# Two layers of graph attention on one core: loads held behind the first x, and the last stage's row sent through memory

## Chip, cores and metric

The kernel runs on one core of one Trainium2 chip. The metric is the device time of one execution in microseconds. The time before is the median of three runs.

## What is computed

Two graph attention layers with a residual connection, on 8 graphs of 1024 nodes and 128 features, all in float32. The adjacency has one entry in 64 set, on average.

```python
def _L0_gnn_ref(h, adj, W, a):
    Wh = jnp.einsum('bni,io->bno', h, W)
    e = (Wh @ a1)[:, :, None] + (Wh @ a2)[:, None, :]
    e = jnp.where(e > 0, e, 0.2 * e)
    attention = jax.nn.softmax(jnp.where(adj > 0, e, neg), axis=2)
    return jax.nn.elu(jnp.einsum('bnm,bmo->bno', attention, Wh))
...
h = jnp.maximum(_layernorm(x, axis=-1), 0.0)
x = x + _L0_gnn_ref(h, adj, L0_gnn_W, L0_gnn_a)
h = jnp.maximum(_layernorm(x, axis=-1), 0.0)
x = x + _L1_gnn_ref(h, adj, L1_gnn_W, L1_gnn_a)
```

The second layer is the same without the elu, with a mask where adj is 0.

## The kernel before

**Stages.** A stage is one layer of one graph, so there are 16, n = 0 to 15. The order is layer 0 of graphs 0, 1, 2, then layer 1 of graph b and layer 0 of graph b + 3 in turn, then layer 1 of graphs 5, 6, 7. LAST is 15. Stages 3 and 15 are LATE (L44): their input x comes out of the stage only three before them.

**One stage.** The 1024 nodes are 8 tiles (t) of 128 rows. For stage n:

- `statistics` and `moments` on VectorE and `normaliser` on GpSimd (a power of -1/2) give the layer norm, `normalise` on ScalarE applies it, `transposes` on TensorE and `copy_hT` on ScalarE turn it (relu on the way).
- `project` multiplies by W, extended by the two columns W a1 and W a2 (`project_a`, `copy_wa`), and gives Wh and the two scores of every node in PSUM (`prj`). `copy_e` takes the scores, `spread_emax` on TensorE and `exp_args` on VectorE take the maximum over all nodes, `exps` on ScalarE the exponentials (`sqr`). `scale_wh` writes Wh into `wh`, scaled.
- The mask of tile t (`masks`, L668, VectorE, 128x1024) is max(row, scalar) min adj: it needs the **row** of the stage, 1024 values that are the same in every partition (`row_r`), a scalar for each partition and the adj tile. `attend` (L950, TensorE) multiplies the masked tile with `wh[t]` into three PSUM banks (`acc`), 8 blocks a tile; each block is two instructions in the trace, so 16 a tile and 128 a stage.
- `take_acc` (the drain, L677 and L687) copies the three banks out on VectorE and takes the reciprocal of the sums. Until bank k is copied, the next stage's first tile can't write it (`acc_copied`). `scale_accs` on ScalarE scales, `add_elu`, `add_x` or `add_hp` on VectorE add to x, and `store` writes layer 1's result out.

**The row.** There are two ways to make it. A stage in `SPREAD = (1, LAST)` uses `spread_r` (L907): eight transposes on TensorE, each of a column broadcast over 128, put the row into PSUM for all partitions, and `copy_row` on ScalarE (L411) copies it to `row_r` in two halves. Any other stage uses `turn_r` (L916), one transpose to 8 x 128, `copy_r` on ScalarE to `rT` (L419), and `load_row` on SyncE (L218): a DMA of 4 KB to memory, a wait until it has landed, and a DMA that reads it back 128 times, 512 KB.

**Order of the work.** Each engine's order is written out by hand. While TensorE works through `attend(n)`, the next stage is prepared between its tiles. For n = 14 the order on TensorE is (L993 to L1014): tile 0, transposes(15), tile 1, project(15), tile 2, spread_emax(15), tile 3, spread_r(15), tiles 4 to 7; then stage 15 with tiles 0 to 3 and `attend_last`, which takes tiles 4 to 7 bank by bank (L959, L965), so that the output leaves in five parts. On VectorE: masks 0 and 1 of stage 14, the drain of 13, masks 2 to 4, copy_e, mask 5, exp_args, the add of graph 5, masks 6 and 7; then (L808 to L813) masks 0 and 1 of stage 15, the drain of 14, masks 2 to 4, the add of graph 6, masks 5 to 7, and `last`. `before_drain(n)` (L188) gives the number of masks of stage n ahead of the drain of n - 1; it is also the tile after which `attend` releases `p_used` (L956).

**The start.** SyncE issues (L231 to L245) the first half of x of graph 0, the three loads of layer 0's weights (w_tr and w_ext, 64 KB each, a_cols, 1 KB), then x of graph 1 and 64 adj tiles of 512 KB with the other x between them. ScalarE's queue issues at the same time (L450 to L454) the second half of x of graph 0 and the three loads of layer 1's weights. TensorE first turns the identity 20 times (`keep_warm`), then `transposes_first`: four tiles that ScalarE has centred, project_a(0), four tiles that VectorE has centred. Then come `project_first`, `project_a(1)` (L974, waits for layer 1's weights), hsum_first of four tiles, spread_emax(0), and so on.

Of the kernel before, what the change touches and what calls it, by code (L numbers as in the profile page):

```python
# [18 lines left out]
def gat_two_layers(nc, x, adj, w0, w0t, a0, w1, w1t, a1, r_rows, out):  # L19
    B, T, _, N = adj.shape  # L20
    D = x.shape[2]
# [4 lines left out]
    HALF = T // 2  # L26
    AHEAD = 3
    X_SLOTS = 6
    LAST = 2 * B - 1
# [14 lines left out]
    LATE = tuple(stage_of[1, b] for b in range(B) if stage_of[1, b] - stage_of[0, b] == 3)  # L44


    SPREAD = (1, LAST)

# [2 lines left out]
    xv = x.rearrange("b (p t) d -> b p (t d)", t=T)  # L53
    ov = out.rearrange("b (p t) d -> b p (t d)", t=T)

    with ExitStack() as ctx:
# [14 lines left out]
        w_ext = sb("w_ext", [P, 2, E])  # L71
        w_tr = sb("w_tr", [P, 2, D])
        a_cols = sb("a_cols", [P, 2, 2])
        adj_sb = sb("adj_sb", [P, AHEAD * T * N], I32)
        x_sb = sb("x_sb", [P, X_SLOTS * T * D])
# [111 lines left out]

        def before_drain(n):  # L188

            return {1: 4, AHEAD: 1, LAST - 2: 3}.get(n, 2)  # L190

        def spread_rows(m):

# [12 lines left out]
        @block.sync  # L206
        def _(sp):
            def load_x(b):
                if b >= X_SLOTS:
                    sp.wait_ge(out_stored[b - X_SLOTS], 16)  # L210
                sp.dma_start(x_at(b), xv[b]).then_inc(x_in[b], 16)

            def load_adj(b, t):
                if b >= AHEAD:
                    sp.wait_ge(p_ready, T * stage_of[1, b - AHEAD] + t + 1)
                sp.dma_start(adj_at(b, t), adj[b, t]).then_inc(adj_in[b % AHEAD][t], 16)

            def load_row(m):  # L218
                k = loaded_rows(m)
                sp.wait_ge(rT_ready, k)  # L220
                sp.dma_start(r_rows, rT[:, :]).then_inc(r_written, 16)
                sp.wait_ge(r_written, 16 * k)
                sp.dma_start(row_r[:, m % 2, :],
                             r_rows.rearrange("t p -> (t p)").partition_broadcast(P)
                             ).then_inc(row_in, 16)

            def store(b):
                sp.wait_ge(hp_free, stage_of[1, b] + 1)
                sp.dma_start(ov[b], x_at(b)).then_inc(out_stored[b], 16)

            sp.dma_start(x_sb[:, 0:HALF * D], xv[0][:, 0:HALF * D]).then_inc(x_half, 16)  # L231
            sp.dma_start(w_tr[:, 0, :], w0t).then_inc(w_in[0], 16)
            sp.dma_start(a_cols[:, 0, :], a0).then_inc(w_in[0], 16)
            sp.dma_start(w_ext[:, 0, 0:D], w0).then_inc(w_in[0], 16)
            load_x(1)
            for t in range(HALF):
                load_adj(0, t)
            load_x(2)
            for t in range(HALF, T):
                load_adj(0, t)  # L240
            for t in range(T):
                load_adj(1, t)
            load_x(3)
            for t in range(T):
                load_adj(2, t)  # L245
            load_row(2)
            load_x(4)
            load_x(5)
            load_row(AHEAD)

            for n in range(AHEAD, LAST):
                l, b = stages[n]
                loads = l == 1 and b + AHEAD < B
                l_old, b_old = stages[n - 3]
                if l_old == 1 and b_old + X_SLOTS < B:
                    load_x(b_old + X_SLOTS)
                if loads:
                    for t in range(3):
                        load_adj(b + AHEAD, t)
                if n + 1 not in SPREAD:  # L260
                    load_row(n + 1)
                if loads:
                    for t in range(3, T):
                        load_adj(b + AHEAD, t)
                if stages[n - 1][0] == 1:
                    store(stages[n - 1][1])
            store(B - 2)
            for k, (lo, hi) in enumerate(last_parts):
                sp.wait_ge(last_ready, k + 1)
                sp.dma_start(ov[B - 1][:, lo * D:hi * D],  # L270
                             x_at(B - 1)[:, lo * D:hi * D]).then_inc(out_stored[B - 1], 16)
            for b in range(B):
                sp.wait_ge(out_stored[b], 16 * (len(last_parts) if b == B - 1 else 1))
# [60 lines left out]
        def _(act):  # L334
# [112 lines left out]
                    nc.scalar.activation(prj[:, k, 0:C], uniform[:, LAST % 2, :],  # L447
                                         ACT.Copy).then_inc(seeded_last, 1)

            half = slice(HALF * D, T * D)  # L450
            nc.scalar.dma_start(x_sb[:, half], xv[0][:, half]).then_inc(x_in[0], 16)
            nc.scalar.dma_start(w_tr[:, 1, :], w1t).then_inc(w_in[1], 16)
            nc.scalar.dma_start(a_cols[:, 1, :], a1).then_inc(w_in[1], 16)
            nc.scalar.dma_start(w_ext[:, 1, 0:D], w1).then_inc(w_in[1], 16)  # L454
            centre_first()
            copy_hT_first()
            exps_first()
# [51 lines left out]
        def _(dve):  # L509
# [145 lines left out]
            def masks(n, tiles):  # L655
                l, b = stages[n]
                for t in tiles:
                    if l == 0:
                        dve.wait_ge(adj_in[b % AHEAD][t], 16 * (b // AHEAD + 1))
                    if n == 0:  # L660
                        dve.wait_ge(row0_ready, 2)
                    elif t == 0:
                        dve.wait_ge(p_used, n)
                        if n in SPREAD:
                            dve.wait_ge(row_copied, 2 * spread_rows(n) + 2)
                        else:
                            dve.wait_ge(row_in, 16 * loaded_rows(n))
                    nc.vector.scalar_tensor_tensor(pbuf[:, t, :], row_r[:, n % 2, :],  # L668
                                                   sqr[:, n % 2, 0, t:t + 1], adj_at(b, t),
                                                   ALU.max, ALU.min).then_inc(p_ready, 1)  # L670
# [136 lines left out]
                    masks(n, (6, 7))  # L807
            masks(LAST, range(before_drain(LAST)))  # L808
            take_acc(LAST - 1)
            masks(LAST, (2, 3, 4))  # L810
            add_hp(B - 2)
            masks(LAST, (5, 6, 7))
            last()  # L813
# [2 lines left out]
        def _(pe):  # L816
# [175 lines left out]
            attend(0, (7,))  # L992
            for n in range(1, LAST):  # L993
                if n + 1 in LATE:
                    k = 1 if n + 1 in SPREAD else 2
                    attend(n, range(k))
                    transposes(n + 1)
                    attend(n, (k,))
                    project(n + 1)
                    attend(n, (k + 1,))  # L1000
                    spread_emax(n + 1)
                    attend(n, (k + 2,))
                    spread_r(n + 1) if n + 1 in SPREAD else turn_r(n + 1)
                    attend(n, range(k + 3, 6))
                else:
                    project(n + 1)
                    attend(n, (0,))
                    spread_emax(n + 1)
                    attend(n, (1, 2) if n + 2 in LATE else (1,))
                    turn_r(n + 1)  # L1010
                    attend(n, (3, 4, 5) if n + 2 in LATE else (2, 3, 4, 5))
                if n + 2 <= LAST and n + 2 not in LATE:
                    transposes(n + 2)
                attend(n, (6, 7))  # L1014
# [33 lines left out]
```

## Time and profile before

| | us |
|---|---|
| median of three runs | 298.88 (298.63 to 299.03) |
| the profiled execution | 298.75 |
| its span | 296.9 |
| what lies around the span | 1.85 |
| TensorE busy | 290.6 (98%) |
| VectorE busy | 268.1 (90%) |
| ScalarE busy | 167.3 (56%) |
| GpSimd busy | 48.5 (16%) |

The profiled execution ran 0.13 us under the median. Busy time is a sum over the span; the chain that ended last, followed back from the last instruction, tells which work set the end. Times in the rows are from the start of the span. "x16" is a count of instructions. TensorE's granted clock is recorded as 1.00 throughout.

### The profile page before, as it was taken

The numbers are of one execution on the slowest core, as the hardware profiler recorded it, in microseconds if no ns is written. First come the engines' busy times: TensorE is split into PE (matmuls) and PEld (weight loads), VectorE is DVE, ScalarE is ACT, GpSimd is POOL, SyncE is SP. The second block draws the span as 40 slices with busy tenths as digits, with TensorE's granted clock in tenths as the row PEclk, the third lists the DMA queues.
The fourth block names the chain that finished last, engine by engine and source line by source line (L and its number), as shares of the span: only waits on it lengthen the run. The fifth ranks groups of instructions, "written<-read, shape, count | busy, mean of one in ns | idle before, by whom it ended". The sixth has DMA issues, their size and how long they took to land.

```text
span 296.9 us, 6592 instructions
## 1 busy us (share of the span) xinstructions
PE 290.6 (98%) x2562; PEld 287.8 (97%) x2562; DVE 268.1 (90%) x613; ACT 167.3 (56%) x490; POOL 48.5 (16%) x53
## 2 busy tenths in 40 slices
PE   7999999999999999999999999999999999999996
PEld 7889999999999999999999999999999999999996
DVE  4796899889999989999899989999899989988796
ACT  3377482983856539382683737566393836384310
POOL 2712003205021120303003030210303000400000
PEclk9999999999999999999999999999999999999999
DMA  7999935004690347714584344903566110101012
GB/s 238 416 408 406 407 148 212 2 7 138 195 371 3 143 153 252 305 33 164 161 305 192 144 128 142 367 8 141 149 227 265 68 77 0 73 0 72 1 73 71
DMA packets 15215, 49.50 MB, mean 167 GB/s; under 512 B 2024, under 2 KB 3280, under 8 KB 15184
## 3 DMA queue, kind: packets, MB, share of 16 engines
q1 hardware_dynamic: 14608, 48.69, 44.4%
q8 instruction: 20, 0.33, 0.4%
q10 hardware_dynamic: 576, 0.39, 0.4%
q14 instruction: 11, 0.09, 0.1%
HBM read 44.83 MB, written 4.25 MB: 165 GB/s over the span
## 4 chain that ended last, share of the span: by engine, by line
PE 86%; DVE 7%; issue 2%; DMA 2%; ACT 2%; POOL 1%; DVEq 0%; POOLq 0%; ACTq 0%
PE acc L950 64%; PE prj L888 8%; PE tp L827 4%; DVE pbuf L668 3%; PE acc L965 2%; PE acc L819 2%; DMA row_r<-r_rows 1%; ACT xn L376 1%; DVE stats L563 1%; PE prj L891 1%; POOL rstd L281 1%; PE prj L860 1%; PE tp L910 1%; DVE accs L677 1%; PE prj L965 1%
## 5 line engine op out<-in xcount | busy, mean ns | idle before, releaser
L950 PE MATMUL acc<-wh,pbuf 128*128 128x129 f32 x1968 | 229.6, 275 | 0.9 <-DVE pbuf L644 0.3
L950 PEld LDWEIGHTS acc<-wh,pbuf 128*128 128x128 f32 x1968 | 225.1, 192 | 1.6 <-issue 0.9
L668 DVE SCALAR_TENSOR_TENSOR pbuf<-row_r,sqr,adj_sb 128x1024 f32<-128x1024 f32 x127 | 157.5, 1276 | 1.4 <-ACT row_r L416 1.0
L281 POOL TENSOR_TENSOR rstd<-vareps,neg_half 128x8 f32<-128x8 f32 x15 | 38.5, 2568 | 202.3 <-DVE vareps L581 202.2
L426 ACT ACTIVATE accs<-accs,rec 128x128 f32<-128x128 f32 x120 | 36.7, 389 | 51.0 <-DVE rec L687 51.0
L376 ACT ACTIVATE xn<-x_sb,shift,rstd 128x128 f32<-128x128 f32 x120 | 47.6, 478 | 0.0
L396 ACT ACTIVATE wh<-prj,wh 128x128 f32<-128x128 f32 x120 | 31.9, 357 | 0.0
L888 PE MATMUL prj<-w_ext,hT 128*128 128x130 f32 x240 | 29.3, 275 | 0.0
L888 PEld LDWEIGHTS prj<-w_ext,hT 128*128 128x128 f32 x240 | 28.0, 191 | 0.0
L382 ACT ACTIVATE hT<-tp 128x1024 f32<-128x1024 f32 x15 | 15.4, 1024 | 20.3 <-PE tp L827 20.3
L677 DVE TENSOR_TENSOR accs<-acc,uniform 128x387 f32<-128x387 f32 (+1 forms) x45 | 20.5, 506 | 2.9 <-PE acc L950 2.8
L563 DVE BATCH_NORM_STATS2 stats<-x_sb 128x6 f32<-128x128 f32 x112 | 22.9, 275 | 0.0
L827 PE MATMUL tp<-ident,xn 128*128 128x128 f32 x128 | 17.4, 277 | 0.3 <-DVE pbuf L668 0.3
L827 PEld LDWEIGHTS tp<-ident,xn 128*128 128x128 f32 x128 | 14.7, 142 | 1.0 <-DVE pbuf L668 0.4
L606 DVE COPY ecol<-prj 128x12 f32<-128x12 f32 x15 | 2.5, 167 | 10.8 <-PE prj L891 10.8
L373 ACT ACTIVATE act_gate<-shift 128x1 f32<-128x1 f32 x15 | 2.9, 192 | 14.1 <-POOL shift L284 14.1
L387 ACT ACTIVATE sqr<-args 128x24 f32<-128x24 f32 x15 | 3.3, 219 | 11.8 <-DVE args L640 11.8
L698 DVE TENSOR_TENSOR x_sb<-x_sb,ex 128x1024 f32<-128x1024 f32 x8 | 9.7, 1217 | 0.1
L692 DVE SCALAR_TENSOR_TENSOR ex<-accs,ex 128x1024 f32<-128x1024 f32 x8 | 9.7, 1218 | 0.0
L438 ACT ACTIVATE ex<-ex 128x1024 f32<-128x1024 f32 x8 | 8.5, 1058 | 0.3
L704 DVE TENSOR_TENSOR x_sb<-accs,x_sb 128x1024 f32<-128x1024 f32 x7 | 8.5, 1218 | 0.0
L436 ACT ACTIVATE ex<-accs 128x1024 f32<-128x1024 f32 x8 | 8.4, 1046 | 0.1
(105 smaller groups left out, 155.6 us busy)
## 6 DMA issues: line engine op xcount, KB each, us to landing
adj_sb<-in_adj SPq DMA_DIRECT2D x64, 512.0 KB, 6.5
row_r<-r_rows SPq DMA_DIRECT2D x13, 512.0 KB, 4.2
x_sb<-in_x SPq DMA_DIRECT2D x7, 512.0 KB, 6.4
out_x<-x_sb SPq DMA_DIRECT2D x7, 512.0 KB, 3.0
x_sb<-in_x ACTq DMA_DIRECT2D x1, 256.0 KB, 3.6
x_sb<-in_x SPq DMA_DIRECT2D x1, 256.0 KB, 3.4
r_rows<-rT SPq DMA_DIRECT2D x13, 4.0 KB
out_x<-x_sb SPq DMA_DIRECT2D x1, 192.0 KB, 1.9
```

Source lines behind the costliest of these rows:

```text
L281: nc.gpsimd.tensor_tensor(rstd[:, :], vareps[:, :], neg_half[:, :], ALU.pow).then_inc(rstd_ready, 1)
L376: nc.scalar.activation(xn[:, t, :], src[:, t, :], ACT.Identity, bias=shift[:, t:t + 1], scale=rstd[:, t:t + 1]).then_inc(xn_ready, 1)
L382: nc.scalar.activation(hT[:, :], tp[:, :], ACT.Relu, accum_out=hsum[:, :]).then_inc(hT_ready, 1)
L396: nc.scalar.activation(wh[:, m % 2, t, 0:D], prj[:, k, s * E:s * E + D], ACT.Copy, scale=wh[:, m % 2, t, D:C]).then_inc(wh_ready, 1)
L426: op = nc.scalar.activation(hp[:, t, :], hp[:, t, :], ACT.Copy, scale=rec[:, t:t + 1])
L563: st = nc.vector.bn_stats(stats[:, t, :], src[:, t, :])
L668: nc.vector.scalar_tensor_tensor(pbuf[:, t, :], row_r[:, n % 2, :], sqr[:, n % 2, 0, t:t + 1], adj_at(b, t), ALU.max, ALU.min).then_inc(p_ ...
L677: nc.vector.tensor_tensor(accs[:, k * NB:k * NB + w, :], acc[:, k, 0:w * C].rearrange("p (s c) -> p s c", c=C), uniform[:, e % 2, :].unsqu ...
L692: nc.vector.scalar_tensor_tensor(ex[:, :, :], hp, 0.0, ex[:, :, :], ALU.max, ALU.subtract).then_inc(hp_free, 1)
L827: return nc.tensor.transpose(tp[:, t * P:(t + 1) * P], xn[:, t, :], ident[:, :])
L888: nc.tensor.matmul(prj[:, k, s * E:(s + 1) * E], hT[:, t * P:(t + 1) * P], w_ext[:, l, :], start=(s == 0), stop=True, skip_group_check=True)
L950: mm = nc.tensor.matmul(sum_at(k, s), pbuf[:, t, i * P:(i + 1) * P], wh[:, n % 2, t, :], start=(t == 0 and s == 0 and k < NB), stop=(t == ...
```

## The change

It does two things. At the start, SyncE issues both halves of the first x, waits until the first has landed, and only then issues everything else; layer 0's weights move to ScalarE's queue and layer 1's to SyncE's, behind the first adj tile. At the end, stage 15 leaves `SPREAD`, so that its row goes through memory (turn_r, copy_r, load_row), and only one of its masks stands in front of the drain of stage 14. The position k = 1 of stage 15's preparation on TensorE is kept.

```diff
-    SPREAD = (1, LAST)
+    SPREAD = (1,)
...
-            return {1: 4, AHEAD: 1, LAST - 2: 3}.get(n, 2)
+            return {1: 4, AHEAD: 1, LAST - 2: 3, LAST: 1}.get(n, 2)
...
-            sp.dma_start(x_sb[:, 0:HALF * D], xv[0][:, 0:HALF * D]).then_inc(x_half, 16)
-            sp.dma_start(w_tr[:, 0, :], w0t).then_inc(w_in[0], 16)
-            sp.dma_start(a_cols[:, 0, :], a0).then_inc(w_in[0], 16)
-            sp.dma_start(w_ext[:, 0, 0:D], w0).then_inc(w_in[0], 16)
+            half = HALF * D
+            sp.dma_start(x_sb[:, 0:half], xv[0][:, 0:half]).then_inc(x_half, 16)
+            sp.dma_start(x_sb[:, half:2 * half], xv[0][:, half:2 * half]).then_inc(x_in[0], 16)
+
+            sp.wait_ge(x_half, 16)
             load_x(1)
             for t in range(HALF):
                 load_adj(0, t)
+                if t == 0:
+                    sp.dma_start(w_tr[:, 1, :], w1t).then_inc(w_in[1], 16)
+                    sp.dma_start(a_cols[:, 1, :], a1).then_inc(w_in[1], 16)
+                    sp.dma_start(w_ext[:, 1, 0:D], w1).then_inc(w_in[1], 16)
...
-            half = slice(HALF * D, T * D)
-            nc.scalar.dma_start(x_sb[:, half], xv[0][:, half]).then_inc(x_in[0], 16)
-            nc.scalar.dma_start(w_tr[:, 1, :], w1t).then_inc(w_in[1], 16)
-            nc.scalar.dma_start(a_cols[:, 1, :], a1).then_inc(w_in[1], 16)
-            nc.scalar.dma_start(w_ext[:, 1, 0:D], w1).then_inc(w_in[1], 16)
+            nc.scalar.dma_start(w_tr[:, 0, :], w0t).then_inc(w_in[0], 16)
+            nc.scalar.dma_start(a_cols[:, 0, :], a0).then_inc(w_in[0], 16)
+            nc.scalar.dma_start(w_ext[:, 0, 0:D], w0).then_inc(w_in[0], 16)
...
             masks(LAST, range(before_drain(LAST)))
             take_acc(LAST - 1)
-            masks(LAST, (2, 3, 4))
+            masks(LAST, range(before_drain(LAST), 5))
...
-                    k = 1 if n + 1 in SPREAD else 2
+                    k = 1 if n + 1 == LAST else 2
```

## Rows read from the trace of the kernel before

**Rows 1.** The page, part 4: the chain that ended last, by engine.
```profile
PE 86%; DVE 7%; issue 2%; DMA 2%; ACT 2%; POOL 1%; DVEq 0%; POOLq 0%; ACTq 0%
```

**Rows 2.** The chain in order of time, 260 to 297 us: start, duration, what.
```profile
271.81 0.87 PE tp L910 x8
272.68 8.49 PE acc L950 x76
...
286.98 5.51 PE acc L965 x48
```

**Rows 3.** Timeline, 246 to 297 us, VectorE: start, duration, instruction, idle before.
```profile
272.00 4.86 DVE L668 SCALAR_TENSOR_TENSOR pbuf<-row_r,sqr,adj_sb 128x1024 f32<-128x1024 f32 x4
...
278.82 1.49 DVE L677 TENSOR_TENSOR accs<-acc,uniform 128x387 f32<-128x387 f32 x3 [1.96 <-PE acc L950]
...
280.47 3.63 DVE L668 SCALAR_TENSOR_TENSOR pbuf<-row_r,sqr,adj_sb 128x1024 f32<-128x1024 f32 x3
...
285.15 3.67 DVE L668 SCALAR_TENSOR_TENSOR pbuf<-row_r,sqr,adj_sb 128x1024 f32<-128x1024 f32 x3
```

**Rows 4.** The chain in order of time, 40 to 52 us: the row of stage 2.
```profile
42.27 0.12 PE tp L918
...
42.71 1.21 DMA r_rows<-rT
...
43.94 4.35 DMA row_r<-r_rows
...
48.42 1.84 DVE pbuf L668 x2
```

**Rows 5.** Broadcast reads (L223), issue to landing: all 13; 100 to 160; 230 to 260.
```profile
DMA to landing us min/median/max: 3.4/4.2/4.8
...
DMA to landing us min/median/max: 4.2/4.2/4.3
...
DMA to landing us min/median/max: 3.4/3.4/3.5
```

**Rows 6.** Timeline, 26 to 78 us: the drain of stage 1 and what follows.
```profile
50.83 1.35 DVE L677 TENSOR_TENSOR accs<-acc,uniform 128x387 f32<-128x387 f32 x3
...
51.52 3.81 PE L950 MATMUL acc<-wh,pbuf 128*128 128x129 f32 x32 [0.21 <-DVE accs L677]
...
52.33 2.43 DVE L668 SCALAR_TENSOR_TENSOR pbuf<-row_r,sqr,adj_sb 128x1024 f32<-128x1024 f32 x2
```

**Rows 7.** Waits of SyncE: us in total, times, longest.
```profile
SPq L223 <- DMA r_rows<-rT: 14.0, 13, 2.2
```

**Rows 8.** Timeline, 0 to 26 us.
```profile
0.72 0.38 SPq L231 DMA_DIRECT2D x_sb<-in_x  x1
...
5.48 1.28 ACT L340 ACTIVATE xn<-x_sb,negmean 128x128 f32<-128x128 f32 x4 [1.59 <-DVE negmean L514]
...
8.63 0.29 DVE L549 BATCH_NORM_STATS2 stats<-x_sb 128x6 f32<-128x128 f32 x1
...
9.67 0.30 PEld L823 LDWEIGHTS acc<-a_cols,w_tr 128*128 128x128 f32 x2
```

**Rows 9.** DMA, 0 to 8 us: GB/s in slices of 0.2 us; issues, median us to landing.
```profile
GB/s 0 0 0 0 0 0 0 0 61 82 82 236 307 399 379 369 420 320 320 259 223 300 205 305 266 274 369 358 379 254 271 287 392 412 389 451 389 389 451 430
...
x_sb<-in_x ACTq DMA_DIRECT2D x1, 256.0 KB, 3.6
x_sb<-in_x SPq DMA_DIRECT2D x1, 256.0 KB, 3.4
...
w_ext<-in_w SPq DMA_DIRECT2D x1, 64.0 KB, 3.9
w_ext<-in_w ACTq DMA_DIRECT2D x1, 64.0 KB, 5.0
```

**Rows 10.** The page, part 6: the small stores of the output, us to landing.
```profile
out_x<-x_sb SPq DMA_DIRECT2D x3, 64.0 KB, 1.6
```

**Rows 11.** The adj load issued at 104.2 us on an idle queue, issue to landing.
```profile
DMA to landing us min/median/max: 3.3/3.3/3.3
```

## The prediction

> **What bounds the kernel now.** I read the page first: the chain that ended last is 86% TensorE, with VectorE next [rows 1]. So an edit pays only where that chain leaves TensorE, or if it takes work off TensorE. Then I read the chain in order of time. At the start it runs through the first x, VectorE, ScalarE and GpSimd. In stage 1 it leaves TensorE for the row of stage 2, which goes through memory. From stage 4 on it is TensorE alone, to the closing matmuls [rows 2]. The change touches the start and the end, so I read those two instruction by instruction.
>
> At the end two engines are level. In the last stage the closing matmuls (L965) need 48 x 0.112 = 5.37 us at the pace of the others (8.49 us for 76) and took 5.51: TensorE already waits some 0.14 us for the last mask [rows 2]. VectorE has an idle 1.96 us ahead of the drain of stage 14, and none between there and its last mask, which ends at 285.15 + 3.67 = 288.82 [rows 3]. A later last mask is a later end, one for one.
>
> **The change at its end: the row of stage 15.** It removes eight transposes (0.87 us of the chain) and puts one in (0.12 as stage 2's turn shows): TensorE reaches the end of stage 14 0.75 us earlier [rows 2, 4]. Two ScalarE copies of half a row become one over 8 partitions, on an engine that is not in the chain there: nothing.
>
> The row, until now copied out of PSUM, takes a round trip. Stage 2 shows each step: from the end of the tile ahead of the turn (42.27) through turn, copy, write (1.21) and broadcast read (4.35) to the first mask at 48.42, that is 6.15 us [rows 4]. In stage 14 the same tile ends at 271.81 [rows 2]. The read's time is the open term. It is 3.4 to 4.8 with a median of 4.2 over the 13 rows; three reads with a load or a store issued within 1 us behind them took 4.2 to 4.3, two with nothing so close took 3.4 and 3.5 [rows 5]. Here the store of batch 5, ready since the add that VectorE ends at 272.0, is queued behind load_row(15) and goes out right behind the read. I take 4.2: the row's mask starts at 271.81 + 6.15 - 0.15 = 277.81.
>
> VectorE has done its two last masks of stage 14 by 272.00 + 4.86/2 = 274.4 and then stands until 277.81, 3.4 us in place of 1.96 [rows 3]. From there its queue is fixed: one mask in front of the drain, 1.21 (half of the 2.41 from 48.42 to 50.83 in stage 2); drain and reciprocal, 1.50 (50.83 to 52.33) [rows 4, 6]; four masks and the add of batch 6, 4.68 (280.47 to 285.15 with three masks) + 1.21 = 5.89; three masks, 3.67 [rows 3]. Sum 12.27, so the last mask ends at 290.08 instead of 288.82: **+1.26 us**. TensorE starts stage 15 at 277.81 + 1.21 + 0.69 = 279.7 (as in stage 2, where the drain starts at 50.83 and TensorE at 51.52) [rows 6], against 272.68 + 64 x 0.112 = 279.83 before, so its 0.75 us is all but spent there. It then waits for mask 1 of stage 15, which has moved behind the drain, and again for the last one. The mask count in front of the drain changes only where TensorE waits; VectorE's total is the same with one or two.
>
> Bounds of this part: with the shortest read, 3.4, the drain waits for TensorE again, mask 1 starts at 280.47 - 0.75 = 279.72 and the last ends at 279.72 + 5.89 + 3.67 = 289.28, +0.46. With 4.8 it is 1.26 + 0.6 = +1.86. For the 13 writes SyncE waited 14.0 us in all, and 2.2 for one of them, 1.2 more than the mean [rows 7]; that would add another 1.2. Neither a gain nor zero comes out, because mask 1 moves behind the drain (1.21) and TensorE gives back only 0.75.
>
> **The change at its start: x alone in front.** The chain begins with the first half of x, issued at 0.72 [rows 8] and landed 3.4 us later. Its other half on ACT's queue, issued at the same moment, took 3.6: the two shared the engines [rows 9]. After the change what shares is w0t, 64 KB, since the second half follows on the same queue. That is 192 KB less ahead of its landing, at some 400 GB/s [rows 9] 0.5 us: it lands at 3.6. Bounds: zero below. Above, a 64 KB store took 1.6 and a single 512 KB load on an idle queue 3.3 [rows 10, 11]; in proportion 256 KB takes 2.33 and lands at 3.05, a gain of 1.1. The kernel's first packets, slow to start, put me nearer to the row of the same load. ScalarE's first activations, four in 1.28 us, and not the opening matmuls, pace the first transposes, so all 0.5 reaches the projection [rows 8].
>
> By the fit in the Trainium skill (DMA: Bandwidth & Descriptors, Anatomy of one DMA: about 2 us and the bytes at 436 GB/s) 256 KB would land at 3.3 and the forecast would be 0.3 us lower; the trace shows 3.4 from issue while two such loads share.
>
> What is held back: x(1) goes out at about 3.7 instead of 2.57. A single load took 3.3 [rows 11], so it lands at 7.0; VectorE wants it at 8.63 - 0.5 = 8.1 [rows 8]. Then come the first adj tile (512 KB at some 410 GB/s, 1.28: 8.3; its mask comes after all of the projection and the row) and the three loads of w1. These were on ACT's queue and landed by 2.12 + 5.0 = 7.1; TensorE wants them at 9.67, in program order ahead of the emax transpose that carries the chain [rows 8, 9]. Their bytes alone take 0.32 us. In pieces of 512 bytes the last of w0's loads landed 1.9 us behind the first half of x, with two full queues around it [rows 9]. I take 0.8: w1 lands at 9.1, wanted at 9.2, so it sits on the edge, and I charge 0.1 (0 to 0.9). The other adj tiles and x(2) land up to 0.7 us later; the second tile lands at 10.4, and its mask runs after the first tile's, behind the row of stage 0. The queue is still clear before stage 2's row write, at 42.71 - 0.4 [rows 4]; if that cover went, stage 2 would pay one for one. w0 on ACT's queue starts earlier than before. **Start: -0.5 + 0.1 = -0.4 us**, and nothing between 28 us and the end takes it back, since everything there follows the chain.
>
> **Sum.** The profiled execution took 298.75 (span 296.9 and 1.85 around it); 298.75 - 0.4 + 1.26 = 299.61. The median of the runs is 0.13 above that execution: 299.7.
>
> **Rivals.** (B) *The row comes as quickly as when nothing is behind it.* A store does not read memory, as the loads did. Read 3.5: the last mask is 1.26 - 0.7 = +0.56 late, and the time is 298.88 - 0.4 + 0.56 = 299.0, no change. For it: the two short reads; against: 4.2 in the one case with a store 1 us behind, the one at 131.9, among the three [rows 5].
>
> (C) *The start gains nothing*: x lands no earlier, or w1 becomes the wait in its place. With w1 at its late end the start costs +0.1 to +0.4, and the time is 298.88 + 1.26 + 0.1 to 0.4 = 300.2 to 300.5. For it: w1's last load was the slowest of the weight loads at 5.0 [rows 9].
>
> The Trainium skill (same page, Queues, rings and completion order) says that a DMA engine drains a whole packet, some 9 to 17 descriptors, from one queue before it turns to the other. A half of x has 8 rows for each engine, so by that rule the two halves would not have shared, x would gain nothing, and the time would be 298.88 + 1.26 + 0.1 = 300.2, case C. The trace speaks against it: the halves landed 0.2 us apart, not the 0.65 that 256 KB take at 400 GB/s.
>
> (D) *The row is later still*, by a read of 4.8 or a slow write: 300.3 to 301.0. Of the 13 rows one read and one write were like this [rows 5, 7].
>
> (E) *Faster*: the first half of x lands at 3.05 and w1 stays in front of its use, so that the start gives 1.09, while the read takes 3.4 and the end costs 0.46: 298.88 - 0.63 = 298.25. It decides only if x lands below 3.1 and the read takes under 3.5, both at the ends of their ranges.
>
> **Numbers.** Chances: forecast 0.42 (299.3 to 300.1), B 0.24, C 0.16, D 0.10, E 0.08. About 0.2%, 0.6 us, is what a measurement can tell from no change. Faster 0.08; within 0.2% 0.30, case B and the low edge of the forecast; slower 0.62. The range 298.6 to 300.8 leaves out E, the upper half of D and a little of C.
>
> **What would show it.** At the start: VectorE's first statistics near 3.65, the emax transpose 0.4 us earlier, and w1's landing beside the second project_a. At the end: one transpose in place of eight, the row's read and its landing time, VectorE idle 3.4 us before mask 0 of stage 15, mask 1 behind the drain, TensorE waiting for the last mask, and 290 - 0.4 for that mask's end. I am wrong if VectorE doesn't wait for the row, if the read takes 3.5, or if TensorE stands at the second project_a.

## The result, and the profile after

The changed kernel takes **301.63 us** (median of 22, 299.74 to 304.55), the kernel before, beside it, 298.85 (22, 298.5 to 301.94): ratio **1.008** [1.0059, 1.010]. The forecast was 299.7 with 298.6 to 300.8. It was 2 us too low, outside the range, with the right sign. Ratios leave out executions over 1.5% above the fastest of their kernel (here the upper two), and are no quotients of the medians.

The executions of one kernel fall into groups, and here the groups are the matter. Of the 22 executions, 11 took 299.7 to 300.9 and 11 took 302.3 to 304.6; in 11, of both groups, TensorE's mean granted clock was 0.989 to 0.994 instead of 1.000. The median, 301.63, is the middle between 300.92 and 302.34, a time that no execution took. Lowest against lowest the change costs 299.74 - 298.50 = 1.24 us.

The profiled execution is one of the quick group: 300.01, span 298.2, clock 1.000. First the page's part 4, the shares of the chain; [rows 1] has 86% TensorE, 7% VectorE and 2% DMA.

```profile
PE 80%; DVE 10%; DMA 4%; issue 2%; ACT 2%; POOL 1%; DVEq 0%; POOLq 0%; ACTq 0%
```

The chain in order of time at the end (start, duration, what; the changed kernel's line numbers are a few higher than before's), against [rows 2]:

```profile
271.58 0.12 PE tp L921
...
271.73 0.28 ACT rT L426
...
272.02 1.20 DMA r_rows<-rT
...
273.24 4.49 DMA row_r<-r_rows
...
279.03 1.36 DVE accs L680 x3
...
280.62 4.74 DVE pbuf L671 x4
285.36 1.14 DVE x_sb L707
286.50 3.60 DVE pbuf L671 x3
...
290.14 3.62 PE acc L968 x30
```

Where TensorE carried the chain through all of stage 15, it now runs turn, write, read, drain and seven masks. The timeline of the same stretch (start, duration, instruction, idle before), against [rows 3]:

```profile
277.82 1.28 DVE L671 SCALAR_TENSOR_TENSOR pbuf<-row_r,sqr,adj_sb 128x1024 f32<-128x1024 f32 x1 [3.57 <-DMA row_r<-r_rows]
...
286.41 3.67 DVE L671 SCALAR_TENSOR_TENSOR pbuf<-row_r,sqr,adj_sb 128x1024 f32<-128x1024 f32 x3
```

```profile
279.72 1.58 PE L953 MATMUL acc<-wh,pbuf 128*128 128x129 f32 x12 [0.89 <-DVE accs L680]
...
281.83 1.61 PE L953 MATMUL acc<-wh,pbuf 128*128 128x129 f32 x12
...
290.14 3.62 PE L968 MATMUL acc<-wh,pbuf 128*128 128x129 f32 x30 [0.26 <-DVE pbuf L671]
```

VectorE stands 3.57 for the row where it stood 1.96. Its last mask ends at 286.41 + 3.67 = 290.08, 1.26 later than before. At the start (timeline, against [rows 8]):

```profile
3.81 0.29 DVE L529 BATCH_NORM_STATS2 stats<-x_sb 128x6 f32<-128x128 f32 x1 [3.81 <-issue]
...
5.12 1.28 ACT L345 ACTIVATE xn<-x_sb,negmean 128x128 f32<-128x128 f32 x4 [1.71 <-DVE negmean L517]
...
5.92 1.03 PE L830 MATMUL tp<-ident,xn 128*128 128x128 f32 x4
...
9.49 0.30 PEld L826 LDWEIGHTS acc<-a_cols,w_tr 128*128 128x128 f32 x2
```

ScalarE starts 5.48 - 5.12 = 0.36 earlier, the second project_a 9.67 - 9.49 = 0.18 earlier. So this execution is -0.18 at the start and 1.26 + 0.18 = +1.44 at the end, +1.26 together. It doesn't show why half of the executions are 3 us longer.

### The profile page after: what moved, and what is told of

Its sections match the earlier page's. It is cut to its first block, busy times and chain, and to the rows that moved or that the text cites. A ratio compares the mean times of both kernels' runs of the same rounds, so it can differ in the third digit from the quotient of the medians.

```text
span 298.2 us, 6579 instructions
## 1 busy us (share of the span) xinstructions
PE 290.6 (97%) x2555; PEld 287.6 (96%) x2555; DVE 268.1 (90%) x613; ACT 166.4 (56%) x489; POOL 49.6 (17%) x53
## 4 chain that ended last, share of the span: by engine, by line
PE 80%; DVE 10%; DMA 4%; issue 2%; ACT 2%; POOL 1%; DVEq 0%; POOLq 0%; ACTq 0%
PE acc L953 60%; PE prj L891 8%; DVE pbuf L671 5%; PE tp L830 4%; DMA row_r<-r_rows 3%; PE acc L822 2%; PE acc L968 1%; DVE accs L680 1%; ACT xn L381 1%; DVE stats L566 1%; PE prj L894 1%; POOL rstd L286 1%; DMA r_rows<-rT 1%; PE prj L863 1%; PE prj L968 1%
```

## The experiments

The expectations name the runs e1 to e16. They are e1 in experiment 1; e2, e13 and e3 in 2; e4 in 3; e5 and e6 in 4; e7 in 5; e11 and e14 in 6; e8, e12, e15 and e16 in 7; e9 and e10 in 8. They were timed in four sets of four, e1 to e4 first, each set on one chip with before beside it: 299.14 (median of 35 executions), 298.97 (27), 298.73 (29), 298.92 (35). A result reads: median in us (lowest to highest, number of executions), then the ratio to before in the same set with its 95% interval. A low clock is a mean granted clock under 0.997.

### 1. The changed kernel once more: what do the long executions do?

> The changed kernel again, for a second trace and for its scatter. Theory R (the row): the loss is the wait of VectorE for the row of stage 15, so it follows the broadcast read. In the profiled execution the read took 4.49 us, VectorE idled 3.57 us and the span grew by 1.3 us against the kernel before. On a chip or in an execution where the time is near 302.5, R expects a row that lands 1.5 to 2 us later (read near 6, or a slow write), the idle at mask 0 of stage 15 longer by as much, and a start that is still some 0.2 us ahead of the kernel before. Rival S (the start): the extra time of such executions sits before 28 us, x or the weights landing later, and VectorE's idle before mask 0 of stage 15 stays near 3.6 us.

300.96 (299.76 to 303.78, 12), 1.0057 [1.0024, 1.0091]: still over the range of the forecast, with 2 or 3 of the 12 in the long group (303.26, 303.78, and 302.12 at a low clock) and 7 at a low clock. The profiled execution is a long one, 303.26 at span 301.5. Its chain, at stage 2's row (compare [rows 4]) and then at stage 15's:

```profile
42.57 2.89 DMA r_rows<-rT
...
45.48 4.56 DMA row_r<-r_rows
```

```profile
274.02 2.55 DMA r_rows<-rT
...
276.58 4.40 DMA row_r<-r_rows
...
289.74 3.60 DVE pbuf L671 x3
```

The 4 KB write takes 2.89 and 2.55 in place of 1.20; the reads are as in the quick execution. The turn of stage 2 is at the same place in both (42.13 and 42.08); behind its late write everything comes 2.0 us later (the turn of stage 15 at 273.58 instead of 271.58), and stage 15's write adds 1.3. That is the 3.3 by which the execution is longer. Late writes make the long group. VectorE's wait ahead of mask 0 of stage 15 is 4.83 instead of 3.57: theory R has the right place, but less than half of the 3.3 arises there, and more at stage 2's row, which neither R nor S had named.

**What holds the write.** Part 3 of the page lists a queue that fetches instructions, here of the changed kernel:

```profile
q8 instruction: 20, 0.33, 0.5%
```

20 packets of 16 KB for TensorE's 2 x 2555 instructions: one for 256. The Trainium skill says the same (Runtime: NRT & Kernel Launch, Instruction fetch mechanics: refilled in 16 KiB blocks of 256 instructions over a DMA queue of the sequencer's own). Now the DMA view from 42.5 to 45.6, 40 slices of 0.0775 us; each packet is booked in the slice in which it starts. The quick execution of the changed kernel, then the long one:

```profile
GB/s 0 0 0 0 0 211 0 0 0 0 40 13 0 0 0 0 0 0 0 0 0 0 0 0 0 0 0 0 53 317 53 317 264 370 370 317 476 264 317 159
...
q8 instruction: 1, 0.02, 2.0%
```

```profile
GB/s 53 0 53 0 0 0 211 0 0 0 20 27 0 0 0 0 0 0 0 0 0 0 7 0 0 0 0 0 0 0 0 0 0 0 0 0 0 0 0 0
...
q8 instruction: 1, 0.02, 2.5%
```

The 211 is the fetch. Its packet takes 2.0% of the time of 16 engines in a window of 3.1 us, so it lasts 0.020 x 16 x 3.1 = 1.0 us (1.2 in the long one). The write goes out in eight pieces of 512 bytes. One piece shows as 6.6 GB/s in its slice, so the eight pieces are the 40 and 13 in the quick execution and the 20, 27 and 7 in the long one. There the lone 7, one piece, starts 0.9 us behind the others, as the fetch ends. At stage 15 the same picture, from 274 to 277:

```profile
GB/s 0 0 0 0 0 0 218 0 0 0 41 7 0 0 0 0 0 0 7 0 0 0 0 0 0 0 0 0 0 0 0 0 0 0 0 0 0 0 0 0
```

**Theory F**: a fetch for TensorE is in flight when the write starts; if it sits on one of the eight DMA engines that the write uses, that piece waits. On the other eight nothing happens. A rival, H: the memory answers late, whatever the queues do.

### 2. The two parts alone

The start alone, with the row of stage 15 by transposes as before:

```diff
-    SPREAD = (1,)
+    SPREAD = (1, LAST)
...
-            return {1: 4, AHEAD: 1, LAST - 2: 3, LAST: 1}.get(n, 2)
+            return {1: 4, AHEAD: 1, LAST - 2: 3}.get(n, 2)
```

> Only the first part of the change: loads held behind the first half of x, row of stage 15 by transposes as before. R: the start's own trace effect alone, 0.1 to 0.4 us faster than before (ratio 0.9985 to 1.000), with the scatter of the kernel before. S: slower than before by 1 us or more in at least some executions, the same upper group of times as the changed kernel.

298.78 (298.43 to 300.86, 12), 0.997 [0.9938, 1.0003]. Repeated in the last set:

> The start alone once more, beside e14 on one chip, since the chip of e9 to e12 showed no low clock in any of 29 executions of the kernel before and so could not tell W from C2. W: more executions with a mean clock under 0.997 than e14 has (a quarter to a half against 0 to 2), and in a traced one with a low clock the second weights landed at 9.5 or later and TensorE stood at the second project_a.

298.90 (298.17 to 301.21, 12), 0.9998 [0.9975, 1.0021]. The start alone makes no difference that can be measured, with 3 and 4 executions of 12 at a low clock, the lowest 0.06 and 0.31 below the lowest of before beside it.

The row alone, with the start as before (and with the change's two lines for the masks and for k):

```diff
-    SPREAD = (1, LAST)
+    SPREAD = (1,)
...
-            return {1: 4, AHEAD: 1, LAST - 2: 3}.get(n, 2)
+            return {1: 4, AHEAD: 1, LAST - 2: 3, LAST: 1}.get(n, 2)
```

> Only the second part: row of stage 15 through memory, one mask in front of the drain, start as before. R: the whole loss and a little more than the changed kernel, +1.3 to +2.8 us, ratio near 1.008 to 1.010, with the wide scatter. S: +1.3 us and no more, with the narrow scatter of the kernel before.

300.25 (299.99 to 303.41, 12), 1.0055 [1.0023, 1.0087]. Nine of 12 lie at 299.99 to 300.56, three at 302.99 or more. The loss is this part's. The ratio is under R's 1.008 to 1.010, and the scatter is not S's narrow one. The profiled execution is of the long kind, with writes of 3.05 and 2.55: the late write needs nothing of the new start.

### 3. The store right behind the read

```diff
                 load_row(n + 1)
...
+                if n + 1 == LAST:
+                    sp.wait_ge(row_in, 16 * loaded_rows(LAST))
```

> The changed kernel with the store of graph 5 held until the row of stage 15 has landed, so that nothing is behind the broadcast read. If the store behind it is what makes the read 4.5 instead of 3.5 us, the read takes 3.4 to 3.7, mask 0 of stage 15 starts 0.8 to 1.0 us earlier and the time falls by 0.7 to 0.9 us against the changed kernel, to 0.3 to 0.6 us above before. If the store does not matter, the read stays at 4.2 to 4.5 and the time stays.

299.73 (299.05 to 303.51, 12), 1.0007 [0.9968, 1.0047]; lowest against lowest of the changed kernel beside it 299.05 - 299.76 = -0.7. The chain shows why:

```profile
273.92 3.67 DMA row_r<-r_rows
```

3.67 in place of 4.49. The read is held up by the store behind it, though a store doesn't read memory, so rival B falls. In five other traces with the store behind it, this read took 4.3 to 4.4.

### 4. Moving the fetches away by empty waits

65 waits in place of TensorE's first one come out as 32 more instructions (6611 for 6579 on the page of the changed kernel, 6624 for 6592 on that of the kernel before), so that every fetch should come earlier in TensorE's work:

```diff
-            pe.wait_ge(const_set, 4)
+            for _ in range(65):
+                pe.wait_ge(const_set, 4)
```

> The changed kernel with 32 empty waits in front of TensorE's first instruction (waits on a count that is there anyway). Theory F (the fetch): TensorE's instructions come in blocks of 16 KB, one fetch for every 256 of them, on one of the DMA engines that also carry the row; where the fetch of about 1 us is in flight on the engine when one of the eight 512-byte pieces of the row write starts (0.76 us after its issue), that write takes 2.5 to 3 us in place of 1.23. It happens at the rows of stage 2 and stage 15 together, in about half of the executions. 32 instructions more in front bring every fetch forward by some 1.8 us of TensorE's stream, so that it is over when the write starts: F expects no time above 301.2, stage 2's and stage 15's writes at 1.23, the fetches at 41.1 and 270.3, and a median of 300.0 to 300.3, at most 1% of a microsecond scatter apart from the group at a clock of 0.994. Rival H (the memory is slow to acknowledge the write in some executions, whatever else runs): the upper group at 302.3 and above stays, in a third to a half of the executions.

303.29 (302.25 to 304.48, 6), 1.0124 [1.0085, 1.0164].

> The kernel before with the same 32 empty waits. F: its own upper group (300.2 to 301.3 at full clock, some 40% of the executions) goes, because only stage 2's write is exposed there and it no longer meets the fetch; median 298.7 to 299.0, and none above 299.4 at full clock. H: the upper group stays.

302.1 (300.87 to 303.27, 10), 1.0082 [1.0054, 1.0110]. The times settle nothing. The waits weren't free: TensorE's first instruction came at 5.07 instead of 1.60, and its opening matmuls entered the chain:

```profile
5.05 4.45 PE acc L819 x20
```

The times spread over 2.2 to 2.4 us, without separate groups. The traces say more. In the kernel before, stage 2's write is issued at 42.71 and the fetch starts at 43.2, so that it is in flight when the pieces start. With the waits the write went out 2.8 us later (45.52) and the fetch only 1.6 later (44.8): between the two the waits shifted 1.2 us, of the 1.8 aimed at. DMA view of the kernel before with the waits, 44.5 to 47.5:

```profile
GB/s 0 0 0 218 0 0 0 0 0 0 0 0 0 0 0 0 0 0 0 0 0 0 0 20 34 0 0 0 0 0 0 0 0 0 0 0 0 0 0 0
...
q8 instruction: 1, 0.02, 2.9%
```

The fetch (218) lasts 0.029 x 16 x 3 = 1.4 us, and all eight pieces (20 and 34) start together, after its end. The write took 1.24. In the changed kernel with the waits it took 1.73 at stage 2, also with no late piece, and 1.22 at stage 15. That fits F; but it is one execution of each, and what made the 1.73 is open.

### 5. Two masks in front of the drain again

```diff
-            return {1: 4, AHEAD: 1, LAST - 2: 3, LAST: 1}.get(n, 2)
+            return {1: 4, AHEAD: 1, LAST - 2: 3}.get(n, 2)
```

> The changed kernel with two masks of stage 15 in front of the drain of stage 14, as in the kernel before. VectorE's queue after the row is the same length, so its last mask should end where it did (290.1 in an execution without a slow write) and the time should be the same within 0.2 us; TensorE should start stage 15 at 280.9 instead of 279.7. If the one mask in front is worth something by itself, this is slower by up to 1.2 us.

301.99 (299.66 to 306.09, 12), 1.005 [1.0009, 1.009]; lowest 299.66 against 299.76 of the changed kernel. VectorE's timeline (the execution is later as a whole by a low clock at its start):

```profile
279.19 2.48 DVE L671 SCALAR_TENSOR_TENSOR pbuf<-row_r,sqr,adj_sb 128x1024 f32<-128x1024 f32 x2 [3.50 <-DMA row_r<-r_rows]
...
287.78 3.67 DVE L671 SCALAR_TENSOR_TENSOR pbuf<-row_r,sqr,adj_sb 128x1024 f32<-128x1024 f32 x3
```

From mask 0 to the end of the last mask 287.78 + 3.67 - 279.19 = 12.26, and 290.08 - 277.82 = 12.26 with one mask ahead. The count of masks is worth nothing, as forecast: TensorE only starts stage 15 later (282.29 - 279.19 = 3.10 behind mask 0 where it was 279.72 - 277.82 = 1.90). The median says nothing on this, since 10 of the 12 executions had a low clock.

### 6. The low clock

Executions at a low mean clock (0.99) are there in the start alone too. The trace of it in windows (us, then busy time of PE, PEld, DVE, ACT, POOL, granted clock, DMA share, GB/s):

```profile
10.00:12.00 2.00, 1.81 (x17) 1.81 (x17) 0.81 (x5) 0.00 (x0) 1.06 (x6) 1.00 0.94 371
12.00:14.00 2.00, 2.00 (x15) 1.81 (x15) 1.29 (x7) 1.06 (x5) 1.76 (x4) 0.80 1.02 410
14.00:16.00 2.00, 2.00 (x11) 2.00 (x10) 1.34 (x4) 1.61 (x6) 0.71 (x2) 0.50 1.03 422
16.00:18.00 2.00, 2.00 (x17) 2.00 (x17) 2.00 (x2) 2.00 (x7) 0.00 (x0) 0.85 1.02 412
```

The clock falls to 0.50, 1.2 instead of 2.4 GHz, for 2 x (0.20 + 0.50 + 0.15) / 0.5 = 3.4 us (the same sum in the three other traces with a low clock), and work at half speed costs up to half of that. TensorE's timeline, ahead of it:

```profile
10.19 0.38 PE L826 MATMUL acc<-a_cols,w_tr 128*128 128x2 f32 x2 [0.54 <-DMA w_ext<-in_w]
```

It stood 0.54 for the last load of w1 (layer 1's weights). Of the traces with this order of loads, the clock fell in four where w1's last load landed at 9.54 to 10.14, and held in three where it landed at 9.17 to 9.51, the changed kernel's among them. **Theory W**: w1, held behind x(1) and an adj tile, comes just about when it is wanted; where it is late, a lower clock follows some 2 to 3 us on. In one of the four, where it landed at 9.54, TensorE hardly stood at all. (Experiment 8 has an eighth trace that speaks against it being certain: w1 at 10.30, a stand of 0.48, and no fall.) The test, on the start alone: w1's three loads in front of the wait for x.

```diff
+            sp.dma_start(w_tr[:, 1, :], w1t).then_inc(w_in[1], 16)
+            sp.dma_start(a_cols[:, 1, :], a1).then_inc(w_in[1], 16)
+            sp.dma_start(w_ext[:, 1, 0:D], w1).then_inc(w_in[1], 16)
             sp.wait_ge(x_half, 16)
...
-                if t == 0:
...
```

> The start alone (as e2), with the three loads of layer 1's weights issued directly behind the halves of x and ahead of the wait, so that only x(1) and the adj tiles are held back. Theory W: in e2, e4 and e7 the last of layer 1's weights landed at 9.5 to 10.1, TensorE stood up to 0.54 us at the second project_a, and 2 to 3 us later its granted clock was at the lower level for some 3.4 us, which costs 0.9 to 1.3 us; the executions with a mean clock of 0.994 are those. With the weights landed by 5.5, W expects a mean clock under 0.997 in no more than 1 or 2 of 12 executions, median 298.4 to 298.7. Rival C2 (the clock falls for a reason of its own, and the new start only has more bad luck): the share stays at a quarter to a half.

298.72 (298.27 to 300.46, 12), 1.0002 [0.9981, 1.0024]. None of 12 at a low clock; 5 of 12 at 299.76 or more, which is stage 2's late write. And in the last set, beside the start alone:

> The start alone with layer 1's weights ahead of the wait. W: a low mean clock in at most 2 of 12, no more than the kernel before on the same chip. C2: as many as e13.

298.60 (297.96 to 300.30, 12), 0.9988 [0.9968, 1.0008]; low clock 1 of 12 against 4 of 12. Over all experiments but those with empty waits: w1 behind the adj tile 42 of 100 executions (11 of 22 of the changed kernel among them), w1 in front of the wait 1 of 48, the start of before 12 of 162. The sets differ (before itself had 5 of 35, 4 of 27, 0 of 29 and 1 of 35); on the two chips where both places of w1 were timed it is 5 of 18 against 1 of 48. So the place of w1's loads sets how often the clock falls; that the stand is what brings it on is not shown.

### 7. Stage 2's row by transposes

On the start alone, and then with w1 in front of the wait as well:

```diff
-    SPREAD = (1, LAST)
+    SPREAD = (1, 2, LAST)
...
-            load_row(2)
...
-                    turn_r(n + 1)
+                    spread_r(n + 1) if n + 1 in SPREAD else turn_r(n + 1)
```

> A candidate against both: the start of the change, the row of stage 15 by transposes as before, and the row of stage 2 by transposes too, so that no row that the chain waits for goes through memory. F: the upper group goes (none above 299.6 at full clock), as no write is exposed; at its best it loses the 0.75 us of seven more transposes and gains back VectorE's wait for the row (0.37) and the start (0.2): 298.6 to 299.2 in nearly all executions, so a lower mean than before but not a lower fastest time. H: the same here, so this run does not separate F from H; it tells whether a better version exists.

298.88 (298.64 to 301.35, 12), 0.9988 [0.9957, 1.0018]; two at a low clock, none else above the first group.

> The candidate: e8 (new start, rows of stages 2 and 15 by transposes) with the weights of layer 1 ahead of the wait. F and W together: neither group is left, all executions between 298.5 and 299.4, and a mean of 298.8, lower than the mean of the kernel before (299.5), at nearly the same lowest time. If either theory is wrong its group shows: near 300.4 for the write, near 299.9 for the clock.

298.81 (298.62 to 299.26, 12), 0.9992 [0.9976, 1.0008]. The chain stays on TensorE where [rows 4] left it:

```profile
41.89 0.87 PE tp L911 x8
42.76 12.51 PE acc L951 x112
```

> The candidate of e12 once more, on this chip: all of 12 executions between 298.5 and 299.4, a mean 0.3 to 0.8 us under the mean of the kernel before, which keeps its two groups.

298.68 (298.56 to 299.01, 12), 0.9978 [0.9957, 1.0000]. The mean is 0.7 under that of before here, and 0.05 under it in e12's set, where before had only 3 of 29 executions in its upper group. What this version gains is the absence of the upper groups, not a lower fastest time. And the edit on the kernel before, with its old start:

> The kernel before with stage 2's row by transposes and nothing else. F: its group near 300.4 is gone; 298.9 to 299.3, so 0.2 above the candidate (the start's share) and a mean under that of the kernel before. If the group stays, the late write of stage 2 was not what made it.

298.99 (298.84 to 299.44, 12), 0.9993 [0.9979, 1.0007]: none above 299.44, where 14 of the 35 of before beside it took 299.79 or more. Without a row write under the third fetch the group of before at some 300.4 is gone.

### 8. The write on all sixteen engines

F says that the eight pieces miss the fetch because they use half of the engines. With 16 rows written instead of 8, none can be missed. The expectation calls this writing the row twice; as built, the first eight rows hold other values of `sqr` and the second eight the row, which is what the read takes. For the traffic this makes no difference. H says that the share of late executions stays.

```diff
-        rT = sb("rT", [T, P])
+        rT = sb("rT", [2 * T, P])
...
-                nc.tensor.transpose(tp[0:T, 0:P], sqr[:, m % 2, 2, :],
+                nc.tensor.transpose(tp[0:2 * T, 0:P],
+                                sqr[:, m % 2, 1:3, :].rearrange("p a t -> p (a t)"),
...
-                             r_rows.rearrange("t p -> (t p)").partition_broadcast(P)
+                             r_rows[T:2 * T, :].rearrange("t p -> (t p)").partition_broadcast(P)
```

> The kernel before with every row written twice (16 lines of 512 bytes in place of 8, so on all 16 DMA engines in place of half of them); the read takes the second copy. Theory F (a fetch of TensorE's instructions in flight on an engine that carries a piece of the write): now any engine that the fetch is on is one of the write's, so stage 2's write is late in nearly every execution where the two overlap in time (all traces so far: fetch 0.4 to 0.5 us after the write's issue, 1 us long, pieces 0.76 us after the issue). Times near 300.4 in 80% or more of the executions instead of 40%; the group at 298.8 all but goes. Theory H (slow acknowledgement of the memory, whatever else runs): the shares stay, 60% near 298.8 and 40% near 300.4.

300.05 (299.73 to 301.93, 12), 1.0037 [1.0017, 1.0057]. All 12 at 299.73 or more; of before beside it 26 of 29 at 299.13 or less. SyncE's timeline, the write and then the read that waits for it:

```profile
42.66 0.34 SPq L221 DMA_DIRECT2D r_rows<-rT  x1
45.35 0.34 SPq L223 DMA_DIRECT2D row_r<-r_rows  x1
```

That is 2.69 us, and VectorE's next mask waits for it, 1.63 where before it waited 0.37:

```profile
49.65 2.48 DVE L668 SCALAR_TENSOR_TENSOR pbuf<-row_r,sqr,adj_sb 128x1024 f32<-128x1024 f32 x2 [1.63 <-DMA row_r<-r_rows]
```

Sixteen pieces are not slow by themselves. The next row of the same execution, with no fetch over it, took 66.89 - 65.53 = 1.36 where eight pieces take 1.22:

```profile
65.53 0.33 SPq L221 DMA_DIRECT2D r_rows<-rT  x1
66.89 0.33 SPq L223 DMA_DIRECT2D row_r<-r_rows  x1
```

On the changed kernel:

> The same edit on the changed kernel. F: stage 2's write late in nearly all executions (+1.7) and stage 15's in most of those where the fetch overlaps it (+1.3): no time under 301, median 303 to 304. H: half of the executions stay at 299.8 to 300.9.

302.19 (301.99 to 304.17, 6), 1.0108 [1.0076, 1.0140]: none under 301.99, writes of 2.52 and 2.17 in the trace. The median is 1 us under the one expected. F holds, H doesn't.

The traces allow a count. In three rows a fetch of TensorE's is regularly in flight when the pieces start: those of stages 2 and 15 and one written at some 130 us (stage 7's). Of such writes in eight pieces 10 of 29 were late, 2.3 to 3.05 us; in sixteen pieces 5 of 5, 2.2 to 2.7. The eight of e9's other eleven writes that took 1.35 to 1.37 had no fetch of TensorE's over them. Of the three late ones, two ran beside adj tiles that were still landing (78.5 and 217.7; some of the quick ones did too), and one beside a fetch of another instruction queue, q14 (235.1).

(w1 landed at 10.30 in this trace and TensorE stood 0.48, and the clock held at 0.999; one of the six had it low.) The Trainium skill (DMA: Bandwidth & Descriptors, Why a DMA increments its semaphore by 16 and not by 1) has the count: a transfer goes over the largest k up to 16 that divides the slowest dimension of both sides. The traces agree: the write of 8 rows shows as 16 packets, 8 pieces and 8 smaller ones, and that of 16 rows as 32.

## Why the prediction was wrong

**The step that failed: the row's write as 1.21, the same in every execution.** It was taken from one row [rows 4], and its other value, SyncE's wait of 2.2 [rows 7], was put into rival D as an accident with a chance of 0.10. It is no accident of the memory but a collision with a fetch of TensorE's instructions, which has its place in the program. With the row of stage 15 through memory it comes in a sixth to a half of the executions (11 of 22 here, 2 to 3 of 12 in experiments 1, 3 and the row alone) and takes stage 2's write and stage 15's together. Stage 2's was already in before (its executions at 300.2 to 301.9, 6 of 22), but the median is one of the other 16; with the change it is joined by a second one on the path. The sum had neither. Lowest against lowest, the +1.24 is inside the range; the long group, some 3 us above that, is outside.

The kernel before could have warned. The wait of 2.2 is the write issued at 129.4, and the DMA view from 129 to 132 shows the fetch (218), seven pieces (20 and 28) and a late one (7), as in the long execution:

```profile
GB/s 0 0 0 0 0 0 0 0 218 0 0 0 0 0 0 20 28 0 0 0 0 0 7 0 0 0 0 0 0 0 0 0 0 0 0 0 0 0 0 0
```

How far the median lies from the forecast is partly luck: 11 long executions of 22 put it between the groups, and 2 or 3 of 12 gave 300.96. The quick executions at full clock, 299.7 to 300.1 and one 300.65, are where the forecast put the kernel.

**Rival C was priced at its stand only.** w1 on the edge, 0 to 0.9, with a chance of 0.16. It landed at 9.25 in the profiled execution (forecast 9.1, wanted 9.2 by the forecast and 9.49 by the trace), so the edge was real. The cost isn't the stand but the clock: low in 42 of 100 executions with this start, for some 3.4 us in each of the four traced, which puts the quick executions about 1 us higher (300.5 to 300.9 in place of 299.7 to 300.1). This term was not in the sum either.

**The end: mechanism right.** Turn, write, read, one mask, drain, four masks, the add, three masks: each step is there. VectorE's stand was forecast as 3.4 and is 3.57; the queue from mask 0 to the last mask 12.27 and 12.26. The absolute times are 0.4 late: mask 0 at 277.81 less the start's 0.4 and at 277.82, the last mask at 290.08 less 0.4 and at 290.08, TensorE's start of stage 15 at 279.7 less 0.4 and at 279.72. The start gave 0.2 less than forecast, and the read took 4.49 for 4.2. The same 0.4 parts the profiled execution, 300.01, from the sum, 299.61. With the store held back the read is 3.67.

**The start: half of the term.** x landed at 0.72 + 3.06 = 3.78 instead of 3.6, a gain of 0.36 at ScalarE and 0.18 at the second project_a. The sentence that ScalarE's first activations, and not the opening matmuls, pace the first transposes was half right. The first transpose starts at 5.93 before and at 5.92 now that its input is 0.36 earlier, because TensorE is in `keep_warm` until then; only the three behind it followed ScalarE, and the group of four takes 1.03 instead of 1.21. E, the faster case, needed x at 3.05 and a read under 3.5, and neither came. The Trainium skill's fit that the prediction sets beside its own term is given there for DMAs that GpSimd issues; SyncE issues this one, and it took 3.06, not the 2.6 of the fit. By the packet rule of the Trainium skill (DMA: Bandwidth & Descriptors, Queues, rings and completion order), as the prediction applies it, x would have gained nothing; the gain of 0.36 speaks against it here, as the rows did.

## What to carry to other kernels

A small transfer through memory on the critical path isn't a constant: look for instruction fetches over it in the DMA view, and take its slow form as a case with its own share, not as a tail. Read several executions before and after; a median between two groups says little, and lowest against lowest and the counts in each group say what changed. A load that lands just in time for TensorE is to be priced with what the clock did afterwards in the executions where it was late. The best version here, with w1 in front of the wait and the rows of stages 2 and 15 by transposes, stayed at 299.26 or below in all 24 executions, while before, beside the experiments, took over 299.5 in 43 of 126.

## What the runs showed of the hardware

- TensorE's instructions are fetched in 16 KB packets, one for 256 instructions, each 0.9 to 1.4 us long in the windows read. A 4 KB write in eight pieces with such a fetch in flight took 2.3 to 3.05 us in 10 of 29 traced writes and some 1.2 in the others; in sixteen pieces 2.2 to 2.7 in 5 of 5, against some 1.36 without a fetch, and none of the 18 executions was a quick one. At stages 2 and 15 the late piece starts 0.4 to 1.0 us behind the others, but the landing is 1.2 to 1.8 later than the usual 1.2: what fills the rest is open.
- In the five traces of the changed kernel and its variants that have both writes in eight pieces and at their usual place to the fetch, both were late (two) or neither (three). Their fetches are the 3rd and the 19th of the kernel, 16 apart. That each next fetch goes to the next of 16 engines, from a place that differs between executions, would explain it; the trace has no numbers of engines, so it is inferred.
- The 512 KB read of stage 15's row took 4.3 to 4.5 in six traces with a store right behind it, and 3.67 in the one with the store held.
- TensorE's granted clock fell to 0.50 for some 3.4 us at 12 to 17 us into the kernel, in executions where w1's last load was late, and once did not although TensorE had stood 0.48 for it: what decides is open.
- Empty waits on TensorE aren't free: 64 more in the program came out as 32 more instructions and put its first matmul (5.07 - 1.60) / 32 = 0.11 us later for each.
- Open: the version with two masks in front of the drain had a low clock in 10 of 12 executions, while the start is the changed kernel's; the start with stage 2 by transposes beside it had 2 of 12.
